# One product of a mixture-of-experts layer moved from VectorE to GpSimd, with a ScalarE copy added

## The reference

```
h_e   = silu(x @ w1[e].T) * (x @ w3[e].T)      e = 0..7, and a ninth, shared expert
y     = sum over e of  combine[token, e] * (h_e @ w2[e].T)   + shared
```

## Time and profile before

| what | us |
|---|---|
| median of 3 runs | 1578.22 |
| lowest and highest of them | 1575.39, 1587.37 |
| the profiled execution, as timed | 1580.4 |
| its span in the profile | 1578.6 |
| PE, DVE, ACT, POOL busy in it | 1250.7, 1038.2, 603.1, 254.3 |

### The profile page before, as it was taken

The page is one execution under the profiler, slowest core; times in us unless marked ns, Lnnn a source line. Parts: engine busy times, 40 slices in busy tenths (PEclk is TensorE's granted clock), DMA queues, the critical chain, the costliest instruction groups (busy, mean ns, idle before and its releaser), DMA issues.

```text
span 1578.6 us, 16492 instructions
## 1 busy us (share of the span) xinstructions
PE 1250.7 (79%) x5768; PEld 754.0 (48%) x5768; DVE 1038.2 (66%) x1997; ACT 603.1 (38%) x992; POOL 254.3 (16%) x205
## 2 busy tenths in 40 slices
PE   0998767799899465769969967678999984657798
PEld 0676433467666122226636753335766641222465
DVE  5656737355666897986646666464565759979764
ACT  5443342444322454432215424344433243454222
POOL 1001000000010363541000010000001014636210
PEclk9999898999999788789979989899999996979899
DMA  6102121000000000000001030300000000000000
GB/s 236 34 21 61 35 60 38 2 1 0 1 0 1 0 1 0 0 0 1 14 29 54 1 94 3 94 3 2 0 1 1 1 0 0 0 0 0 1 7 14
DMA packets 23543, 32.05 MB, mean 20 GB/s; under 512 B 3008, under 2 KB 19168, under 8 KB 22880
## 3 DMA queue, kind: packets, MB, share of 16 engines
q1 hardware_dynamic: 23456, 30.94, 6.7%
HBM read 23.40 MB, written 8.06 MB: 20 GB/s over the span
## 4 chain that ended last, share of the span: by engine, by line
PE 58%; DVE 23%; issue 7%; DMA 6%; ACT 5%; SPq 1%; POOL 1%; DVEq 0%; POOLq 0%; ACTq 0%
PE bank L1221 11%; PE bank L1223 10%; PE bank L1222 10%; PE bank L1383 7%; DVE n_h L1188 5%; DVE a_mx L1126 3%; PE bank L1294 3%; PE bank L1230 3%; DVE bank L1180 3%; DMA X<-in_x_dram 2%; PE bank L1440 2%; PE bank L1480 2%; PE bank L1348 2%; DMA a_k<-stack_dram 2%; PE bank L1421 2%
## 5 line engine op out<-in xcount | busy, mean ns | idle before, releaser
L991 DVE SCALAR_TENSOR_TENSOR f_hl<-bank,f_hh 128x512 fp32r<-128x512 f32 x192 | 131.8, 689 | 128.8 <-ACT f_hh L695 127.9
L695 ACT ACTIVATE f_hh<-bank 128x512 fp32r<-128x512 f32 x192 | 114.8, 598 | 207.0 <-PE bank L1294 206.6
L623 POOL TENSOR_TENSOR n_hc<-n_h,n_cs 128x512 f32<-128x512 f32 x128 | 160.6, 1272 | 127.7 <-DVE n_h L1188 79.1
L749 ACT ACTIVATE m_sl<-bank 128x512 f32<-128x512 f32 x144 | 85.9, 598 | 233.2 <-PE bank L1223 232.8
L1221 PE MATMUL bank<-xT_h,mw_h 128*128 128x512 f32 x288 | 162.7, 565 | 5.4 <-DVEq L433 4.3
L570 POOL TENSOR_TENSOR small<-small,half 128x4 f32<-128x4 f32 x24 | 24.3, 1013 | 829.5 <-DVE small L894 829.0
L1530 PE MATMUL bank<-n_hc,ident 128*128 128x512 f32 x256 | 145.8, 690 | 11.0 <-POOL n_hc L623 10.3
L1051 DVE TENSOR_TENSOR m_t<-m_sl,bank 128x512 f32<-128x512 f32 x128 | 87.8, 686 | 99.2 <-PE bank L1223 85.1
L1188 DVE TENSOR_TENSOR_SCAN n_h<-n_da,bank 128x512 f32<-128x512 f32 x128 | 149.5, 1203 | 5.0 <-POOL n_hc L623 4.9
L825 ACT ACTIVATE n_da<-n_dt,amat 128x512 f32<-128x512 f32 x128 | 91.7, 721 | 144.1 <-DVE n_h L1188 124.3
L1383 PE MATMUL bank<-m_h,mw 128*128 128x512 f32 x288 | 145.4, 593 | 0.0
(11 more groups left out here) (241 smaller groups left out, 2488.7 us busy)
## 6 DMA issues: line engine op xcount, KB each, us to landing
w_stage<-in_mw_dram SPq DMA_DIRECT2D x16, 256.0 KB, 2.7
a_q<-stack_dram SPq DMA_DIRECT2D x8, 512.0 KB, 6.2
a_k<-stack_dram SPq DMA_DIRECT2D x16, 256.0 KB, 7.7
stage_fw<-in_fw_dram SPq DMA_DIRECT2D x2, 1536.0 KB, 9.9
stack_dram<-R SPq DMA_DIRECT2D x16, 192.0 KB, 2.8
stack_dram<-R SPq DMA_DIRECT2D x16, 128.0 KB, 2.5
stage_b<-in_bias_dram SPq DMA_DIRECT2D x1, 1728.0 KB, 10.1
X<-in_x_dram SPq DMA_DIRECT2D x5, 256.0 KB, 2.8
```

The lines of the kernel that those rows point to most:

```text
L623: n_hcs.by(nc.gpsimd.tensor_tensor(n_hc[:, m, :], n_h[:, m, :], n_cs[:, n // 2 % 2, :], ALU.mult))
L695: f_hi.by(act.activation(f_h[0][:, i % 4, :], bank[:, i % 3, :], ACT.Relu))
L991: f_lo.by(V.scalar_tensor_tensor(f_h[1][:, i % 4, :], bank[:, i % 3, :], 0.0, f_h[0][:, i % 4, :].bitcast(F32), ALU.max, ALU.subtract))
```

## The change

ACT copies the combine row of an expert from PSUM to a new SBUF tile `m_c` (ring of two), once per routed expert, between silu of the expert's even half and what follows. POOL makes `m_t = m_sl * m_c`, at each of the 16 routed steps, ahead of the piece of preparation of that step. DVE makes one product per step, `m_h = m_t * B_i`. A product of three factors is taken in another order; nothing else is computed.

The waits change with it. A_i on PE now waits for silu of step i-2 instead of DVE's first product of that step. B_i, which followed A_i without a wait of its own, now waits for `m_h` of step i-2 (it is the last reader of the bank). The combine row waits for the copy of the row two experts back instead of a DVE product. POOL's product waits for silu, for the copy and for `m_h` two steps back.

```diff
@@ sb / sig
+        m_c = sb("m_c", [P, 2, T], F32, s)
+        m_cc = sig("m_cc", "moe", EXPERTS)
@@ gpsimd
                         for i in range(MSTEPS):
+                            if i < 2 * EXPERTS:
+                                pool.wait_ge(m_silu.sem, m_silu.at(k, i))
+                                pool.wait_ge(m_cc.sem, m_cc.at(k, i // 2))
+                                if i >= 2 or p == 1:
+                                    pool.wait_ge(m_hs.sem, m_hs.at(k, i - 2))
+                                m_ts.by(nc.gpsimd.tensor_tensor(m_t[:, i % 2, :], m_sl[:, i % 2, :],
+                                                                m_c[:, i // 2 % 2, :], ALU.mult))
                             hand_over(u, i - MOE_LAG * p)
@@ scalar
-                        if i >= 2:
+                        if 2 <= i < 2 * EXPERTS + 2:
                             act.wait_ge(m_ts.sem, m_ts.at(k, i - 2))
                         elif p == 1:
                             act.wait_ge(m_hs.sem, m_hs.at(k, i - 2))
                         m_silu.by(act.activation(m_sl[:, i % 2, :], bank[:, i % 2, :], ACT.Silu))
+                        if i % 2 == 0 and i < 2 * EXPERTS:
+                            e = i // 2
+                            act.wait_ge(m_cr.sem, m_cr.at(k, e))
+                            if e >= 2:
+                                act.wait_ge(m_ts.sem, m_ts.at(k, 2 * e - 3))
+                            m_cc.by(act.activation(m_c[:, e % 2, :], bank[:, 4 + e % 2, :], ACT.Copy))
@@ vector
-                    dve.wait_ge(m_silu.sem, m_silu.at(k, i))
+                    if e < EXPERTS:
+                        dve.wait_ge(m_ts.sem, m_ts.at(k, i))
+                    else:
+                        dve.wait_ge(m_silu.sem, m_silu.at(k, i))
@@
-                        m_ts.by(V.tensor_tensor(m_t[:, i % 2, :], m_sl[:, i % 2, :], bank[:, 2 + i % 2, :], ALU.mult))
-                        dve.wait_ge(m_ts.sem, m_ts.at(k, i))
-                        dve.wait_ge(m_cr.sem, m_cr.at(k, e))
-                        m_hs.by(V.tensor_tensor(m_h[:, i % 3, :], m_t[:, i % 2, :], bank[:, 4 + e % 2, :], ALU.mult))
+                        m_hs.by(V.tensor_tensor(m_h[:, i % 3, :], m_t[:, i % 2, :], bank[:, 2 + i % 2, :], ALU.mult))
@@ tensor
-                        if i >= 2:
-                            pe.wait_ge(m_ts.sem, m_ts.at(k, i - 2))
-                        elif p == 1:
+                        if i >= 2 or p == 1:
+                            pe.wait_ge(m_silu.sem, m_silu.at(k, i - 2))
+                        m_a.by(product(bank[:, i % 2, :], [mw[c][:, e, m, :] for c in range(2)], x))
+                        if i >= 2 or p == 1:
                             pe.wait_ge(m_hs.sem, m_hs.at(k, i - 2))
-                        m_a.by(product(bank[:, i % 2, :], [mw[c][:, e, m, :] for c in range(2)], x))
                         m_b.by(product(bank[:, 2 + i % 2, :], [mw[c][:, e, 2 + m, :] for c in range(2)], x))
@@
                             if e >= 2:
-                                pe.wait_ge(m_hs.sem, m_hs.at(k, i - 3))
+                                pe.wait_ge(m_cc.sem, m_cc.at(k, e - 2))
```

## The result

| | before | after |
|---|---|---|
| median of 6 runs each, us | 1579.05 | 1619.11 |
| lowest and highest | 1575.39, 1587.37 | 1615.69, 1623.85 |
| profiled execution, and its span | 1580.4, 1578.6 | 1617.56, 1615.8 |

The ratio is 1.0245, with an interval of 1.0212 to 1.0279: the change costs 40 us, 37.2 by the spans. The mean granted clock of the after execution is 0.921.

What follows compares the result with a forecast made beforehand. PE was taken as the bound (58% of the chain). Moe pairs of 10.3 before mamba and 7.8 last, twice each, give 36.2; less 1.4, +35 on 1580.4 is 1615, and 1613 as median; range 1598 to 1630.

Steps and rivals of the forecast that it cites:

- "exp": Even unit: PE waits 0.8, 0.4, 0.15 and 0.4 us at B_11 to B_14; with restarts +2.8.
- POOL's pace there: In the exp stretch of an even unit, POOL delivers a product each 2.9 us against PE's mean 2.37.
- steps 4 to 6: Unit 6, ordinary steps: the longer path fits behind PE's work, so no waits.
- Opening: Start of an even unit: PE idle about 1.7 us each ahead of B_2 and B_3; +3.1 us.
- The router and the end of the unit: Even unit: router's product at step 7 waits 0.5 plus restart, +0.8 us; at the end DVE is held, +0.4.
- The odd units: Each odd unit +0.7 us at B_2; before mamba +2.5 more, with waits of 1.2 at B_5 and 1.0 at B_7.
- Half clock: In two openings PE already runs at half clock, which hides part of the chain through POOL: -1.4 us.
- Everything fits: Products ready before PE reaches B_3 and B_11 to B_14; gains 6 us of PE's waits, about 1570; chance 7%.
- POOL and DVE hold each other up throughout: POOL's product at 1.6 us or more in every step, h_i later too; 1628 to 1645; chance 9%.
- The clock falls: New gaps drop PE's clock inside units; ten us at half clock in "exp" of four units adds 20, 1633; 4%.

Runs made afterwards that it cites:

- e1_exp_later: Changed kernel with POOL's four exp powers after the products of steps 9, 10, 11 and 13 instead of 8 to 11: 1607.72 us, ratio 1.0156 to before.
- e4_cheap_powers: Changed kernel with every POOL power of a moe unit replaced by a same-shape multiplication of constants, same place and waits: 1601.54 us, ratio 1.0124 to before.
- e9_half_product: Changed kernel with POOL's product made for 256 of 512 columns only, DVE reading that half twice: 1592.12 us, ratio 1.0072 to before.
- e6_copy_only: Kernel before, with ACT copying the combine row and DVE's second product reading the copy: 1582.49 us, ratio 1.0014 to before.
- e7_split_wait: Kernel before, with only PE's waits moved as in the change, all products on DVE: 1578.52 us, ratio 0.9991 to before.
- e3_both_later: Changed kernel with POOL's exp powers and its inverse-root power for the next unit both placed after later products: 1602.63 us, ratio 1.0124 to before.
- e5_pool_beside: Kernel before, plus an unread POOL product of the changed kernel's shape at each of 16 routed steps: 1595.27 us, ratio 1.0102 to before.

## Why the prediction was right

The forecast of 1613 was on the right side, by the mechanism named, and 6 us short of 1619.11. By its own steps (in the row of unit 6's pieces, measured is by how much PE's delay against the kernel before grows over each piece):

| step | predicted | measured |
|---|---|---|
| PE's wait at B_2, B_3 (unit 6) | 1.7 each | 1.77, 1.76 |
| router's product at step 7 | 0.5 + restart | 0.38 + 0.27 |
| waits in "exp", even unit | 0.8, 0.4, 0.15, 0.4 | 0.66, 0.30, 0.08, 0.30 |
| POOL's pace there | 2.9 | 2.84 |
| waits before mamba: B_2, B_5, B_7 (unit 7) | 0.45, 1.2, 1.0 | 0.36, 1.22, 1.00 |
| POOL's product | 1.25 | 1.28 |
| steps 4 to 6 | no wait | none |
| unit 6: opening, router, "exp", end | +3.1, +0.8, +2.8, +0.4 | +3.0, +0.65, +2.4, +0.7 |
| an even unit at the full clock | +7.1 | +6.8 |
| half clock, all units | -1.4 | +0.6 |
| four even units | +27.0 | +27.8 |
| two odd units before mamba | +6.4 | +6.9 |
| two last units | +1.4 | +1.3 |
| all eight units | +34.8 | +36.0 |

**Opening.** B_2 and B_3 were both late, and the releaser was `m_h`. Of PE's 0.51 wait ahead of A_2 and its restart, which the change removes, little came back: h_0 was late by more than A_2 came earlier, as the step had it.

**The router and the end of the unit.** The router's wait was 0.38 for 0.5, and with its restart of 0.27 this term was 0.8 predicted and 0.65 measured. At the end of the unit the predicted 0.4 was 0.7: a wait of 0.19 with a longer first pair (1.13 in place of 0.86), and 0.2 ahead of it at the "weights" piece of PE.

**"exp".** Four waits, as predicted, each about 0.1 smaller; the alternation of product and power ran at 2.84, not 2.9. `e1_exp_later` and `e4_cheap_powers` show that POOL's order and the powers' length make these waits, and `e9_half_product` that 0.55 us less in the product removes them too.

**The odd units.** The waits before mamba came to 2.58 us in all, against 2.65 predicted. The third one the prediction put down to "rows" on DVE between h_4 and h_5, with 0.8 of it for operations held by POOL's products, after the earlier trace rows. DVE's and PE's timelines in unit 7 bear out the place and give less to the hold:

```profile
483.84 0.55 DVE L888 TENSOR_TENSOR small<-small 128x4 f32<-128x4 f32 x1
...
488.00 0.69 DVE L1070 TENSOR_TENSOR m_h<-m_t,bank 128x512 f32<-128x512 f32 x1
...
488.74 0.50 PE L1237 MATMUL bank<-xT_h,mw_h 128*128 128x512 f32 x1 [1.00 <-DVE m_h L1070]
```

B_7 starts when h_5 is done, and h_5 starts when "rows" is. One operation of "rows" is held, 0.55 in place of 0.16; the others have their lengths of before. So about 0.4 of the 1.00 is contention, half of what was taken, and the rest is the 3.8 us of "rows" itself, which now stand on the way of B_7. No run took the hold out alone.

**Half clock.** The term of -1.4 rested on two openings at half clock, 711.5 to 716.1 and 1193.9 to 1197.3 before. They made these two units 1.1 and 0.6 us longer than the same units of the other pair. After, three stretches of the eight units ran at half clock, each 3 to 5 us long. One row of each (stretch, length, PE, PEld, DVE, ACT, POOL, clock, DMA, GB/s):

```profile
721.00:722.00 1.00, 1.00 (x3) 0.81 (x4) 0.00 (x0) 0.00 (x0) 0.00 (x0) 0.50 0.00 0
1222.00:1223.00 1.00, 1.00 (x4) 0.81 (x3) 1.00 (x5) 0.00 (x0) 0.00 (x0) 0.50 0.00 0
1522.00:1523.00 1.00, 1.00 (x3) 0.64 (x3) 0.00 (x0) 0.37 (x1) 0.94 (x1) 0.50 0.00 0
```

The first is the opening of unit 10 in pair 1. There B_2's wait is 0.37 in place of 1.77, so the half clock hides most of the wait for the path through POOL, as the step said. The unit as a whole is 0.7 longer than unit 10 of pair 2, where it was 1.1 longer before, so of its price only 0.4 is hidden:

```profile
727.39 0.50 PE L1237 MATMUL bank<-xT_h,mw_h 128*128 128x512 f32 x1 [0.37 <-DVE m_h L1070]
```

The other two lie inside a unit, behind these waits. In unit 6 of pair 2 PE waits 1.76 and 1.75 at B_2 and B_3, and 0.9 us after the second the granted clock falls to 0.50, from 1220.4 to 1223.9:

```profile
1215.03 0.50 PE L1237 MATMUL bank<-xT_h,mw_h 128*128 128x512 f32 x1 [1.76 <-DVE m_h L1070]
...
1219.55 0.50 PE L1237 MATMUL bank<-xT_h,mw_h 128*128 128x512 f32 x1 [1.75 <-DVE m_h L1070]
```

From A_0 to the router's product this unit takes 24.01 us and unit 6 of pair 1, with the same waits at the full clock, 22.36: 1.65 us for it, not hidden. In unit 10 of pair 2 the slow matmuls (1520.8 to 1524.2) come just where B_3 would have waited; 0.12 of that wait is left, and the time to the router's product is 22.36, as at the full clock. So the step was right that half clock can hide the new waits, and wrong on where it would be. All told, half clock costs the even units 2.3 us after and 1.7 before: the term came out at +0.6 and not -1.4, of the other sign. At the full clock the four even units are 1.2 us less late than forecast. These two misses offset each other, so that 27.0 stands so near 27.8 is in part luck.

The new waits are not shown to bring the clock down. Stretches of this kind, 3.4 to 5 us long, lie in the first 15 us of even units of every kernel: in two of four before and in `e6_copy_only`, in all four of `e7_split_wait`, where no projection waits for a product of DVE, and in one of four of `e3_both_later`. No odd unit has one. Why one opening gets it and the next does not, no run here settles.

**Outside the units.** The spans differ by 1.2 us more than the units, and the medians by 3 more than the spans. For the profiled execution the forecast was 1580.4 + 34.8 = 1615.2 and the time 1617.56: 2.4 us short, half of it in the units. The other 3.7 of the 6 come from taking the median 2.2 below the profiled execution, as it was before; after, it lies 1.5 above. The runs of each kernel lie 8 to 12 us apart, so this part is no term of the mechanism, and that the total came so near owes something to it too.

**The rivals.** *Everything fits* fell: PE waits for `m_h` 27 times. Its prize was also put too high: the 6.1 us are idle time of the weight loads (PEld), while PE's matmuls waited for `m_t` only 1.0 us in the whole program. *POOL and DVE hold each other up throughout* fell as stated, with a mean product of 1283 ns and none over 1303, where it wanted 1600; its mechanism exists, as `e5_pool_beside` shows at 13 to 19 us, but it needs POOL products without pauses. *The clock falls* is not borne out: half-clock stretches inside the units are there before and after, their price rose by 0.6 us where the rival had 20, and none lies in "exp". Unit 6 of pair 1 over its length, as in the earlier trace rows, kept the full clock:

```profile
417.00:471.00 54.00, 48.47 (x180) 29.84 (x181) 20.69 (x54) 18.28 (x30) 27.58 (x21) 1.00 0.00 1
```

DVE is busy for 20.69 of 54 us (38%), POOL for 27.58 (51%), and the granted clock is 1.00: both have room in a unit that is 6.8 us longer.

**What none of the repairs reached.** With the powers moved and DVE doing the opening the median is 1595.74, still 15 above the kernel before (0.9% to 1.3%). The path silu, copy, POOL, DVE is longer than the one it replaces. What the change removes is small: PE's matmuls waited 1.0 us in all for DVE's product, and their loads 6.1. The new waits at B_2 and B_3 alone are 12.4 us on the matmuls.

## What to carry to other kernels

Before work goes to an idle engine, write down its list in order, and lay the new piece beside each small one in it: at 26% busy POOL still stood behind 27 waits of PE. In 17 of them (B_3, B_11, B_12 and B_14 of the even units, B_5 of the odd ones before mamba) a power and its wait for DVE stood ahead of a product that PE needed. The eight at B_2 come from the length of the new path, at the start of a unit where PE has nothing else to do meanwhile, and the two at B_7 from DVE's own list. Compare the pace of the mixed stretch (1.28 + 1.64) with the pace of the bound (2.37), not the busy shares. And look first at what the relieved engine was worth: DVE lost 81 us of work here, and PE's matmuls had waited 1.0 us, their loads 6.1, for the product that the change moves.

## What the runs showed of the hardware that was not expected

- A small DVE operation that has two SBUF operands, or that only reads and writes SBUF with a scalar (L882), lasts until POOL's running product ends: 1.04 to 1.22 us for 0.16 in `e5_pool_beside`, 0.55 in the changed kernel. DVE's products with a PSUM operand are not held (687 ns). Unpaced POOL work beside a schedule with such operations cost 13 to 19 us; 64 more ACT copies cost -1 to +6 by the interval.
- On POOL a power is dear against a product of the same size: 1639 ns and 202 ns for 128x8, 1.01 us for 128x4. A 128x512 product took 1283 ns, a 128x256 one 732; on a straight line through these two, about 180 ns do not scale with the size.
- A wait of PE ahead of a matmul of 512 columns cost here 0.27 us more than its length, behind a pause of 0.08 us as behind one of 1.77.
- Behind two waits of 1.76 us with four us of work between them PE's granted clock fell from 1.00 to 0.50 in one unit and stayed at 1.00 in another of the same program; it fell as well in units without these waits, four times in `e7_split_wait`.
